# Attention steps on one Trainium2 core: q and k split in two parts for the scores, the fourth query tile transposed within its own step, values after the next scores, VectorE's layernorm and routing work spread over the steps

## The reference

```python
latent_kv = x @ w_kv_down
kv = latent_kv @ w_kv_up
k, v = (kv[..., :HD], kv[..., HD:])
q = (x @ w_q).reshape(Bx, Tx, N_HEAD, HEAD_SIZE)
att = jnp.einsum('bqhd,bkhd->bhqk', q, k) * scale
att = jnp.where(causal, att, -jnp.inf)
att = jax.nn.softmax(att, axis=-1)
y = jnp.einsum('bhqk,bkhd->bqhd', att, v)
...
x = x + _L0_attn_ref(_layernorm(x, axis=-1), ...)
x = x + _L0_ffn_ref(_layernorm(x, axis=-1), ...)
```

## Time and profile before

| | us |
|---|---|
| runs | 951.78, 951.95, 955.58 (median 951.95) |
| the profiled execution, its own time | 954.19 |
| its span, first to last instruction | 952.4 |
| PE busy in the span | 898.0 |
| DVE busy | 616.8 |
| ACT busy | 585.8 |
| POOL busy | 543.1 |

### The profile page before, as it was taken

One profiled execution on the slowest core, in us unless ns is written; L12 is line 12 of the kernel. 1 busy time (PEld: TensorE's weight loads), 2 busy tenths in 40 slices (PEclk: granted clock), 3 DMA queues, 4 the chain that ended last, 5 costly groups with the idle time before them and its releaser, 6 DMA issues.

```text
span 952.4 us, 19227 instructions
## 1 busy us (share of the span) xinstructions
PE 898.0 (94%) x5614; PEld 619.5 (65%) x5615; DVE 616.8 (65%) x2378; ACT 585.8 (62%) x1486; POOL 543.1 (57%) x536
## 2 busy tenths in 40 slices
PE   6899999999999999999999999999851999999996
PEld 3566666666666666666666666665531888888885
DVE  3666677777767777776776677677854454455453
ACT  3676777677667766776676677667631555544553
POOL 3555564666466556646655764665553466666555
PEclk9999999999999999999999999999985999999999
DMA  7765410000000000000000000000011233333332
GB/s 201 279 280 225 147 47 1 7 12 18 1 14 19 5 7 12 18 1 13 20 3 7 13 18 1 12 20 4 3 32 34 37 48 47 46 46 44 44 45 28
DMA packets 43991, 44.29 MB, mean 47 GB/s; under 512 B 4352, under 2 KB 35968, under 8 KB 43920
## 3 DMA queue, kind: packets, MB, share of 16 engines
q0 software_dynamic: 16528, 26.03, 11.3%
q1 hardware_dynamic: 27392, 17.39, 6.6%
HBM read 15.28 MB, written 28.12 MB: 46 GB/s over the span
## 4 chain that ended last, share of the span: by engine, by line
PE 91%; issue 4%; DVE 2%; ACT 1%; POOL 1%; SPq 0%; POOLq 0%; DMA 0%; DVEq 0%
PE low_ps L979 15%; PE low_ps L967 9%; PE mid_ps L903 8%; PE low_ps L1130 7%; PE mid_ps L905 6%; PE mid_ps L904 6%; PE out_ps L986 6%; PE mid_ps L946 6%; PE top_ps L946 5%; PE top_ps L967 4%; PE low_ps L946 4%; PE out_ps L1122 4%; PE top_ps L903 2%; PE top_ps L905 2%; PE top_ps L904 2%
## 5 line engine op out<-in xcount | busy, mean ns | idle before, releaser
L328 POOL TENSOR_TENSOR prob<-prob,row_inv 128x512 f32<-128x512 f32 (+3 forms) x256 | 321.3, 1255 | 283.1 <-DVE row_inv L639 281.0
L460 ACT ACTIVATE prob<-prob,neg_max 128x256 f32<-128x256 f32 (+3 forms) x512 | 280.9, 551 | 172.8 <-DVE neg_max L632 172.8
L979 PE MATMUL low_ps<-PT,v_sb 128*64 128x512 f32 (+3 forms) x1024 | 151.9, 439 | 2.4 <-ACT PT L466 2.4
L415 POOL DMA_INDIRECT out<-prob,meta_row x71 | 110.9, 1562 | 35.9 <-issue 34.8
L979 PEld LDWEIGHTS low_ps<-PT,v_sb 128*64 128x64 f32 x1024 | 67.8, 136 | 94.0 <-issue 64.9
L967 PEld LDWEIGHTS low_ps<-ident,prob 128*128 128x128 f32 x768 | 86.4, 140 | 60.1 <-issue 50.9
L967 PE MATMUL low_ps<-ident,prob 128*128 128x128 f32 x768 | 108.3, 277 | 3.1 <-DVE neg_max L632 2.4
L860 DVE TENSOR_TENSOR prob<-mid_ps,prob 128x512 f32<-128x512 f32 x71 | 49.1, 692 | 90.4 <-ACT prob L563 74.1
L460 ACT ACTIVATION_READ_ACCUMULATOR prob<-prob,neg_max 128x1 f32 x512 | 96.7, 189 | 0.0
L632 DVE CUSTOM_DVE_ANT_0 prob<-mid_ps,mask 128x128 f32<-128x128 f32 (+1 forms) x256 | 93.6, 421 | 1.6 <-PE mid_ps L946 0.8
L632 DVE CUSTOM_DVE_ANT_0 prob<-top_ps,mask 128x512 f32<-128x512 f32 x128 | 83.2, 688 | 11.7 <-PE low_ps L967 11.6
(11 more groups left out here) (172 smaller groups left out, 1699.8 us busy)
## 6 DMA issues: line engine op xcount, KB each, us to landing
routed_rows<-W_dn POOLq DMA_DIRECT2D x8, 2080.0 KB
routed<-routed_rows SPq DMA_DIRECT2D x71, 65.0 KB
X<-in_L_attn_x SPq DMA_DIRECT2D x8, 256.0 KB, 5.5
W_ffn<-in_L_ffn_Wg SPq DMA_DIRECT2D x8, 256.0 KB, 5.7
W_ffn<-in_L_ffn_Wu SPq DMA_DIRECT2D x8, 256.0 KB, 6.9
W_dn<-in_L_ffn_Wd SPq DMA_DIRECT2D x8, 256.0 KB, 4.6
out<-X SPq DMA_DIRECT2D x8, 256.0 KB, 2.3
out<-prob,meta_row POOLq DMA_INDIRECT x71
```

The source lines that it names most:

```text
L328: nc.gpsimd.tensor_tensor(p_pair(i), p_pair(i), row_inv[:, i, :].unsqueeze(2).to_broadcast([P, 2, P * (i + 1)]), ALU.mult).then_inc(S["nor ...
L415: nc.gpsimd.indirect_dma_start(out=out, out_offset=bass.IndirectOffsetOnAxis(ap=meta_row[:, q:q + 1], axis=0), in_=eo_sb[q], in_offset=Non ...
L460: nc.scalar.activation(p_at(i, h), p_at(i, h), ACT.Exp, bias=neg_max[:, i, h:h + 1], scale=-1.0, accum_out=row_sum[:, i, h:h + 1]).then_in ...
L979: last = nc.tensor.matmul(y_ps[h * HD:(h + 1) * HD, j * P:T], v_sb[:, half, j, o + h * HD:o + (h + 1) * HD], PT[:, h, j, j:NT, :].rearrang ...
```

## The change

q and k get a high and a low part: `qk_sb` has a part index and is fp32r. ACT writes the high parts in two instructions of 512 columns (`qk_hi`), DVE the low parts in two (`qk_lo`), and each score tile becomes three fp32r matmuls a head (high x high, high x low, low x high) accumulated in PSUM, where it was one fp32 matmul a head. Tile 3 is transposed at the end of its own step, into `top_ps`, with tile 2 in `low_ps`. Values of step n-1 follow the scores of step n directly. `y_copy` moves from DVE to ACT. POOL norms all four tiles in a row and issues its scatters after them. DVE's layernorm and routing pieces are cut into smaller ones, each put either behind the inverse of tile 2 or behind the copy of transposed tile 0. The expert weights' split is spread one expert to a step, two in steps 54 and 55, three in steps 61 to 63, three in the tail. `xn_sb` goes to unused blocks of PT and `xn2T` shares `outT`. The core of the diff:

```diff
-        qk_sb = sb("qk_sb", [P, 2, T])
+        qk_sb = sb("qk_sb", [P, 2, 2, T], F32R)
...
+        SPLIT_AT = {STEPS - 10: 1, STEPS - 9: 5, STEPS - 3: 0, STEPS - 2: 4, STEPS - 1: 2}
+        SPLIT_END = [6, 3, 7]
...
 (POOL, step)
-                if n:
-                    norm(n - 1, 3)
-                norm(n, 1)
-                norm(n, 0)
-                norm(n, 2)
+                for i in ORDER:
+                    norm(n, i)
+                if post is not None and k in SCATTERS:
+                    scatter_at(post, k)
...
 (ACT)
-            def qk_copy(n):
-                seen(act, S["qk_ready"], n + 1)
-                nc.scalar.activation(qk_sb[:, :, :].rearrange("p a n -> p (a n)"), mid_ps[:, :], ACT.Copy).then_inc(S["qk_copied"], 1)
+            def qk_hi(n):
+                for a in range(2):
+                    seen(act, S["qk_ready"], 2 * n + a + 1)
+                    nc.scalar.activation(qk_sb[:, 0, a, :], mid_ps[:, a * T:(a + 1) * T], ACT.Copy).then_inc(S["qkhi_done"], 1)
+            def y_copy(n):
+                seen(act, S["y_ready"], n + 1)
+                nc.scalar.activation(y_sb[:, :], y_ps, ACT.Copy).then_inc(S["y_copied"], 1)
...
+                    exps(n, 2)
+                    exps(n, 3)
+                y_copy(n - 1)
+                if nxt:
+                    qk_hi(n + 1)
...
+                if n in SPLIT_AT:
+                    split_hi(SPLIT_AT[n])
+                if v:
+                    v_copy(n + 3, (k + 3) % NP // NT, (k + 3) % NT)
+                if cur:
+                    t3_copy(n)
...
 (DVE)
+            def qk_lo(n):
+                for a in range(2):
+                    seen(dve, S["qkhi_done"], 2 * n + a + 1)
+                    nc.vector.tensor_tensor(qk_sb[:, 1, a, :], mid_ps[:, a * T:(a + 1) * T], qk_sb[:, 0, a, :].bitcast(F32),
+                                            ALU.subtract).then_inc(S["qklo_done"], 1)
...
+                    inv(n, 2)
+                if n - 1 in SPLIT_AT and cur:
+                    split_lo(SPLIT_AT[n - 1])
+                if pre is not None and k == 1:
+                    pre_stats(pre)
...
                 if cur:
-                    inv(n, 2)
-                if prev:
-                    y_copy(n - 1)
+                    inv(n, 3)
+                    t_copy(n, 1)
+                if nxt:
+                    qk_lo(n + 1)
                 if cur:
-                    t_copy(n, 1)
-                    inv(n, 3)
+                    t_copy(n, 2)
                     t_copy(n, 0)
-                    t_copy(n, 2)
+                if post is not None and k == 2:
+                    post_stats(post)
...
 (PE)
-                for h in range(2):
-                    d = slice(h * HD, (h + 1) * HD)
-                    last = nc.tensor.matmul(scores_at(i, h), qk_sb[d, 0, i * P:(i + 1) * P], qk_sb[d, 1, 0:P * (i + 1)],
-                                            start=True, stop=True)
+                for k, (a, b) in enumerate(((0, 0), (0, 1), (1, 0))):
+                    for h in range(2):
+                        d = slice(h * HD, (h + 1) * HD)
+                        last = nc.tensor.matmul(scores_at(i, h), qk_sb[d, a, 0, i * P:(i + 1) * P], qk_sb[d, b, 1, 0:P * (i + 1)],
+                                                start=(k == 0), stop=(k == 2))
...
+                if i == 2:
                     seen(pe, S["t1_copied"], n + 1)
...
-                if prev:
-                    transposes(n - 1, 3, cur)
+                values(n - 1, (k - 1) % NP, cur)
                 if nxt:
                     project(n + 1, (k + 1) % NP, m + (k + 1) // NP)
-                if prev:
-                    values(n - 1, (k - 1) % NP, cur)
-                if v:
-                    seen(pe, S["qk_copied"], n + 2)
-                    v_chunk(n + 3, m + (k + 3) // NP, (k + 3) % NP // NT, (k + 3) % NT)
...
+                project_out(n - 1, (k - 1) % NP)
+                if cur:
+                    transposes(n, 2)
+                if v:
+                    seen(pe, S["qklo_done"], 2 * n + 3)
+                    v_chunk(n + 3, m + (k + 3) // NP, (k + 3) % NP // NT, (k + 3) % NT)
+                if cur:
+                    transposes(n, 0)
+                if cur:
+                    transposes(n, 3)
```

More of the change, by code:

```diff
@@ new lines, in step @@
+                if n - 1 in SPLIT_AT and cur:
[3 more added lines that the diff above has]
+                if post is not None and k == 2:
+                    post_x2(post)
+                if pre is not None and k == 3:
+                    pre_norm(pre)
+                if post is not None and k == 4:
+                    post_xn2(post)
+                if post is not None and k == 5:
+                    post_choose(post)
@@ L685, in split_weights @@
[L685 to L690 removed]
+                if post is not None and k == 2:
+                    post_stats(post)
+                if post is not None and k == 3:
+                    post_aggr(post)
@@ new lines, in step, with split_lo @@
+                if pre is not None and k == 3:
+                    pre_lo(pre)
+                if post is not None and k == 5:
+                    post_chosen(post)
+                if post is not None and k == 6:
+                    post_rows(post)
+            def split_lo(e):
+                dve.wait_ge(S["split_hi"], SPLIT_ORDER.index(e) + 1)
+                nc.vector.tensor_tensor(up_lo[:, e, :], W_ffn[:, e, :], up_hi[:, e, :].bitcast(F32), ALU.subtract)\
+                    .then_inc(S["split_lo"], 1)
@@ L772, in _ @@
             dve.wait_ge(S["base_set"], 1)
-            maxes(0, 1)
-            maxes(0, 0)
-            maxes(0, 2)
+            qk_lo(0)
+            for i in (1, 0, 2):
+                maxes(0, i)
             inv(0, 1)
@@ L911, in pre_T @@
                 for t in range(NT):
-                    last = nc.tensor.transpose(xT_ps(b)[:, t * P:(t + 1) * P], xn_sb[:, t, :], ident[:, :])
+                    last = nc.tensor.transpose(xT_ps(b)[:, t * P:(t + 1) * P], xn_sb[t], ident[:, :])
                 last.then_inc(S["xT_ready"], 1)
@@ L970, in values @@
             def values(n, pair, cur):
-                seen(pe, S["t3_copied"], n + 1)
-                for i in range(NT - 1 if not cur else 0):
+                if cur:
+                    seen(pe, S["max_done"], 8 * (n + 1) + 2)
+                for i in range(NT if not cur else 0):
                     seen(pe, S[f"t{i}_copied"], n + 1)
@@ L1016, in step @@
                     pre_T(pre, m)
-                if prev:
-                    project_out(n - 1, (k - 1) % NP)
+                project_out(n - 1, (k - 1) % NP)
[4 more added lines that the diff above has]
+                    v_chunk(n + 3, m + (k + 3) // NP, (k + 3) % NP // NT, (k + 3) % NT)
                 if cur:
                     transposes(n, 0)
-                    transposes(n, 2)
+                if post is not None and k == 4:
+                    post_logits(post)
+                if cur:
+                    transposes(n, 3)
             def post_out(b):
                 seen(pe, S["outT_copied"], b + 1)
+                seen(pe, S["routing"], ROUTING * (b - 1) + 14)
                 for t in range(NT):
@@ L1077, in _ @@
                 v_chunk(t, 0, 0, t, t % 2)
-            for i in (1, 0, 2):
+            for i in (1, 2, 0):
                 transposes(0, i)
```

189 lines of the change are left out of this document (74 added, 115 removed).

## The result

The changed kernel takes 947.48 us (median of 5 runs, 945.86 to 950.33), the kernel before 953.95 in 5 runs on the same chip: ratio 0.9939, 95% interval 0.9917 to 0.9961. It is faster by 0.6%: 6.5 us where 24 were forecast. The profiled execution took 950.33 us, its span 948.5.

What follows compares the result with a forecast made beforehand. PE, busy 94% of the span, was taken as the bound. 63 steps -15.8, projection stalls -1.8, last batch's stalls -3.3 and tail -3.0 sum to -23.9: span 952.4 to 928.5, median forecast 928, range 918 to 950.

Steps and rivals of the forecast that it cites:

- the plain step: A step without layernorm or routing on PE: 9.95 us instead of 10.20, from scores -0.20, order -0.10, a wait +0.05.
- the rival of the narrow pass: Tile 0's 128-column fp32r passes cost as much as fp32: +0.31 us a step, 947.5 in all; chance 0.13.
- The wait before tile 2: New wait of tile 2's transposes for tile 1's copy, as both use low_ps: +0.05 us a step.
- The heads run side by side: Assumed for the fp32r scores; the rival that they no longer do: +1.7 us a step, about 1050; chance 0.05.
- weight loads stay hidden: Assumed for the score passes; the rival of exposed loads: +0.85 us a step, about 998; chance 0.04.
- a gap of 1.3 us: On DVE between tile 2's inverse (+4.6) and tile 3's (+5.9), for layernorm and routing pieces, costed at nothing.
- the 0.6 us of slack: Tile 3's normalisation ready at +8.5 us into a step, PE reaching its transposes at +9.1.
- a wait takes the saved time: Rival: a barely met wait is missed by 0.2 us, making steps 10.15: +12.6, 941; chance 0.15.
- the -3.3 for the last batch: Idle before the maxima behind the weights' split, 0.60 + 0.22 us, gone in four steps of the last batch.
- the tail: From the last step's scores to the last output projection: 17.4 us becomes 14.3, called -3.
- Routing table and expert tiles: nothing changes, 0: The work after the steps, routing table and expert tiles, was to keep its time: 0.
- opening 0: Less to stream at 1.2 GHz against one more dependence, low parts before v: 0, within 1 us either way.

Runs made afterwards that it cites:

- scores_fp32: The changed kernel with scores again as one fp32 matmul a head, high and low parts still made; 959.54 us, ratio 1.0029.
- poolfree: The changed kernel with POOL's normalisation of tile 2 cut to 2 columns a head in the 14 layernorm steps, rest unnormalised; 939.80 us, ratio 0.9826.
- place: The changed kernel with DVE's layernorm pieces moved to where POOL does not norm; 940.46 us, ratio 0.9865.
- stt: The changed kernel with both layernorms' instruction written as scalar_tensor_tensor instead of tensor_scalar; 950.26 us, ratio 0.9951.
- splits: The changed kernel with one expert weights' split a step earlier and the two of the last two steps in the tail; 951.77 us, ratio 0.997.
- combo: place plus the edits of splits, plus tile 1's copy ahead of tile 3's inverse in step 0; 940.05 us, ratio 0.9849.
- best: final plus, in the tail, POOL's reciprocal deviation of the last batch after four of the scatters instead of all; 939.83 us, ratio 0.9834.
- final: combo with the scatters two a step, in four steps of a batch; 935.82 us, ratio 0.9792.
- after_again: The changed kernel unaltered, measured again; 951.74 us, ratio 0.9961.
- before_split: The kernel before with only the q/k split into high and low parts, step order kept old; 975.74 us, ratio 1.0215.

## Why the prediction was right and wrong

**Right: the plain step.** 9.95 forecast and measured, though the terms are less exact than their sum. Scores 2.16 forecast, 2.09 measured. Tiles 0 and 2 together were 0.33 + 0.54 and took 0.85, so a pass of 128 columns costs about what the transpose row said, and the rival of the narrow pass falls. The wait before tile 2 was put at 0.05: the output projection's block takes 1.04, 0.18 over its 0.86. Against it, tile 2's transposes take 0.60 where 0.75 stood in the sum. Nor do the halves come out as forecast: scores_fp32 puts the split at 0.24 a plain step (0.20 forecast) and leaves 0.01 for the order (0.05 forecast). Tile 3 was to be normed 0.6 us ahead of PE: the normalisations end at 282.77, PE comes at 283.34. The heads run side by side (12 matmuls of tiles 0 and 2 in 0.85 us), and weight loads stay hidden.

**Wrong: "The layernorm and routing pieces ... a gap of 1.3 us ... I cost it at nothing, and what overruns the gap takes from the 0.6 us of slack first".** I took the durations from the old places on DVE, 349 ns in the mean, and did not ask what POOL does in the new place. It runs the normalisations of tiles 0 and 2 there without a pause, and one instruction of the four is held for nearly the whole of the second. The four take 2.56 us, which do not fit in 1.3: in step 27 the inverse of tile 3 comes 6.92 after the step's start, where +5.9 was worked out. Nor does the overrun take from the slack first, as the prediction has it. It meets PE earlier, at a wait that the prediction's list does not have: PE's transposes of the layernorm's own result (L934, L1055), which start +7.06 into step 27 of the changed kernel and +6.35 in poolfree. Tile 3 is not late in that step:

```profile
311.63 1.90 POOL L333 TENSOR_TENSOR prob<-prob,row_inv 128x1024 f32<-128x1024 f32 x1 [0.50 <-DVE row_inv L646]
```

```profile
314.45 1.04 PE L984 MATMUL top_ps<-ident,prob 128*128 128x128 f32 x8
```

Its normalisation ends at 313.53, PE comes at 314.45. Price: 0.8 in each of 14 steps, 11.2 us, shown by poolfree (hold shortened, 632.46 us from step 1 to 63) and by place (order changed, k = 3 and k = 4 the same as poolfree's). With it the sum would have been -12.7. The rival "a wait takes the saved time" named the right kind of cost, but at the wrong place (the values' copy on ACT) and in all steps. That the narrow-pass rival's 947.5 is what was measured is chance: its mechanism is not there.

The Trainium skill (SBUF — State Buffer, "Who interferes with whom") has the rule I left out: VectorE in a 2-port mode, which tensor_scalar can enter, or with two SBUF inputs, and GpSimd exclude each other, and the later one waits for the whole of the other's instruction. The traces agree: 1507 ns, up to within 0.1 us of the end of a normalisation that had started just before, and in stt the two-input form at a mean of 684. Which mode tensor_scalar runs in, no run here shows.

**Wrong: two pieces in one gap.** In step 55 the split (1.20 us) and the routing weights stood in one gap, in which one cast took 1.22 us (the same cast takes 0.39 in the last step of splits), and PE idled 1.33 before tile 2: part of the -3.3 for the last batch was given back here and in step 63. splits shows it: 11.27 to 10.04. The sum of steps 1 to 63 in poolfree, where this stall stayed, still met the forecast, in part by luck: its steps k = 3 to 5 together are 1.5 us shorter than before, twice the 0.25 a step that was worked out.

**Wrong: the tail.** -3.0 was forecast from the last scores to the last output projection; measured is 695.32 - 679.94 = 15.4 against 17.4, so -2.0. The missing 1.1 are the expert weights' splits in the last two steps, on which the prediction puts no price there: with these moved into the tail, splits, combo, best and final have the 14.3 that was worked out. PE before tile 2 of the last step in the changed kernel, an idle that these four don't have:

```profile
688.66 0.84 PE L984 MATMUL low_ps<-ident,prob 128*128 128x128 f32 x6 [1.34 <-DVE PT L651]
```

(In four other profiles the number is 16.3 to 16.6, with 3.4 us at a granted clock of 0.50 there.) And 1.6 of the gain were lost again behind the projection, 1.4 of them before the transposes of the last layernorm:

```profile
703.95 1.12 PE L1055 MATMUL post_ps<-ident,routed 128*128 128x128 f32 x4 [6.17 <-DVE routed L733]
```

The kernel before idles 4.73 there. Now all 8 scatters of batch 6 stand behind POOL's last normalisation (from 690.21, the last at 700.42 for 0.96), and the reciprocal deviation behind them starts at once, at 701.40; before, where two of them came earlier, POOL had waited 2.77 for DVE's variance when it started it. "Routing table and expert tiles: nothing changes, 0" left out the stretch between.

**Wrong: opening 0 and expert tiles 0.** In the two profiles they are +4.1 and +1.8. Neither can be laid to the change alone. Step 1 began between 31.56 and 36.27 in the twelve profiles of the changed order, with PE's speed after the first idle as the largest part. At like speed the change does cost something there. after_again came to full speed at nearly the same time as the kernel before (21.1 and 21.3 us), and its step 1 began at 34.05 against 32.18: 1.9 us, outside the "within 1 either way". Of that 1.2 are the wait for the low parts, the step of dependence that the prediction named. The kernel before, then after_again:

```profile
24.01 0.50 PE L903 MATMUL mid_ps<-Wb,XT 128*128 128x512 f32 x1 [0.25 <-ACT qk_sb L454]
```

```profile
25.03 0.50 PE L925 MATMUL mid_ps<-Wb,XT 128*128 128x512 f32 x1 [1.42 <-DVE qk_sb L657]
```

The expert tiles took 220.1 in the profile of the kernel before, 220.4 to 224.1 in those of the changed order, and 222.6 in before_split, whose order is the old one. Busy time by stretches of 4 us (PE, PEld, DVE, ACT, POOL, then the granted clock) from the expert tiles' start, before_split, then the kernel before:

```profile
751.90:755.90 4.00, 3.06 (x8) 2.27 (x9) 0.58 (x2) 2.35 (x4) 0.00 (x0) 0.50 0.22 52
755.90:759.90 4.00, 3.36 (x11) 2.38 (x10) 1.07 (x4) 1.13 (x4) 0.00 (x0) 0.50 0.07 17
759.90:763.90 4.00, 4.00 (x20) 3.66 (x19) 1.47 (x5) 1.27 (x3) 0.19 (x1) 0.65 0.00 0
```

```profile
732.30:736.30 4.00, 3.20 (x8) 2.41 (x9) 0.58 (x2) 2.43 (x4) 0.00 (x0) 0.50 0.24 52
736.30:740.30 4.00, 3.36 (x20) 2.49 (x19) 1.66 (x5) 1.47 (x3) 0.00 (x0) 0.91 0.06 17
```

0.50 is the 1.2 GHz level; the kernel before left it some 4 us earlier than before_split. What decides that was not tested.

**The sum.** Against the forecast span of 928.5 the profile's 948.5 is 20.0 too long: 11.1 in the steps, 4.1 in the opening, 2.6 in the tail, 1.8 in the expert tiles, and 0.3 of the 63rd step, which the stretches above don't count. With the pieces placed, and with the edits of scatters, splits and opening that the forecast did not have, final is 18.5 us under the kernel before, of 24 forecast.

## What to carry to other kernels

A duration is a property of an instruction and of what runs on the neighbouring engine: when a reordering moves VectorE's SBUF-only work, look up what GpSimd does in the new gap, place it where GpSimd is idle, and list who waits for its result. A split that costs an extra stage pays only in an order that gives this stage room; test both halves alone before crediting either, and look whether a half still carries a stall of its own. Before a tail is reordered, name who waits for the landing of what is put later.

## What the runs showed of the hardware

- An fp32 tensor_scalar of 128x128 on VectorE, SBUF to SBUF, 0.33 us alone, lasted up to 1.51 us beside a GpSimd tensor_tensor of 1.46, and both ended within 0.1 us, in 14 steps of 14. scalar_tensor_tensor on the same operands is held as well (684 ns in the mean). Where GpSimd was idle, the mean was 341.
- A maximum of scores in PSUM against a mask in SBUF came 0.9 to 1.2 us late, at the end of a GpSimd indirect DMA, in some executions of a kernel and not in others; in steps k = 8 the scatter stood at the same relative time within 0.1 us in both. In the three profiles with the scatters moved, no maximum was later than 0.4 us. Whether the instruction or its semaphore was held, and whether the chip decides, is open.
- fp32r matmuls of 64 rows and 128 columns ran two heads side by side at about 0.1 us a pass; this is an estimate, from 0.85 for tiles 0 and 2 less 0.54 for the three passes of tile 2.
- After an idle of 1.4 us in the opening, the next matmuls of the same opening ran at full speed in one execution and at about half in another.
